# A graph network kernel: the second attention pass with the bias in the products, sigmoid from PSUM, an early running sum and three filler products a round

## The chip, the cores and the metric

The kernel runs on one core of one Trainium2 chip. The time is the device time of one execution in microseconds (us). It is given as the median of several runs.

The core has five engines with queues of their own: TensorE (PE; its weight loads are PEld), VectorE (DVE), ScalarE (ACT), GpSimd (POOL) and SyncE (SP). They wait for each other through semaphores. SP issues nearly all plain DMAs; POOL issues the indirect ones (rows by index).

## The reference

100,000 nodes with 128 channels, 50,000 edges sorted by destination, all float32. The input is normalised, goes through three layers of graph attention, is added back, normalised again, and goes through three layers of a second network (GIN). The change lies in the attention layers only:

```
h = x @ W;  s = h @ a_src;  d = h @ a_dst
e = leaky(s[src] + d[dst])                  # one score for each edge, and for each node's self loop
w = exp(e - e_max[dst]);  denom = segment_sum(w, dst)
alpha = w / (denom[dst] + 1e-16)
out = segment_sum(alpha[:, None] * h[src], dst) + bias
x = x + sigmoid(out)
```

Nodes without an incoming edge are computed in a dense pass of their own; what follows is for the nodes that have one.

## The kernel before

The work is done in stages, one behind the other. First a dense pass over all nodes computes the three attention layers as if no node had an incoming edge. Then, for each attention layer m = 0, 1, 2, two passes over the edges correct the nodes that have one: a first pass gathers the source rows by index and computes scores (only for m = 1 and 2; for m = 0 it lies beside the dense pass), a short chain on slabs of 98 x 512 makes maxima, sums and weights, and a second pass makes new node rows. The stages of the second network follow. The change touches the second pass. It is run three times and is called pass 0, pass 1 and pass 2 below.

A pass has R = 49 rounds. A round has U = 8 columns of 128 edges. `p2_round(i, ...)` is written once for each engine; in turn i an engine works on several rounds at once, as the names say: `inside(i - 1)` guards the part of the turn that is for round i-1. The order of the work is the order in which these parts are written: nothing is scheduled. `p_rounds` writes out the first three and the last turns and loops over four turns at a time between them. A round goes like this:

- DVE `early_fields` copies keys and weights of a round. PE `keys_along` (L1297) turns the keys along the free axis, eight transposes; DVE `masks` (L1792) compares them, which gives a 0/1 matrix with weights (tile pA, whose buffers are bNE and aH). ACT `diagonals` (L1047) makes eight diagonal matrices (bSW).
- PE sums the edges of a node within a column: L1311 (source rows bXs times mask) and L1312 (own rows pXd times diagonal), 8 each, into PSUM banks 2 and 3. ACT copies them to pAT (L1064).
- A node whose edges spill over a column's end needs the sum so far. DVE keeps it as a running sum pC, one scan over the last columns (L1823, L1626), round after round. PE multiplies it with W (L1305), ACT copies the 8 rows to pCW (L1053).
- One turn later PE makes the output: L1321 (pAT times W) and L1323 (an indicator matrix, tile pIN in the buffer aO, which has 1 where an edge of column u takes the carried sum u, times pCW), 8 each, into banks 4 and 5.
- DVE L1830 multiplies with 1/denom (pFL) and adds the bias (GB), eight instructions; ACT L1070 takes the sigmoid, two instructions of 512; DVE L1846 adds the old rows; POOL L864 scatters the rows by index.
- In passes 0 and 1 DVE also makes the scores of the next layer from these rows a turn later (L1808, L1810, sixteen reductions, then the copy L1814). In pass 2 DVE, POOL and ACT make the next normalisation instead (L1851 to L1863, L873 to L877, L1059).

A float32 product is run on PE as two matmuls, each with a weight load of its own, and a transpose as one. SP loads rows, indicators and stores results, each turn.

Of the kernel before, what the change touches and what calls it, by code (L numbers as in the profile page):

```python
# [22 lines left out]
P = 128  # L23
# [21 lines left out]
def gnn_program(nc, x, src, dst, attr, Ws, a_src, a_dst, gat_b, enc_w0, enc_b0, w1_0, b1_0, g_0, be_0, rm_0,  # L45
# [38 lines left out]
    ind_d = dram("ind_d", (R, U, U * P))  # L84
    gat_src = [x, x1_d, x2_d]
# [3 lines left out]
    with ExitStack() as ctx:  # L89
# [152 lines left out]
        def pair_ends(p):  # L242
# [57 lines left out]
        l_xr = sems("l_xr", 2)  # L300
        l_st = sems("l_st", 2)
        (p_fe, p_fl, p_kt, p_A, p_dg, p_ag, p_ev, p_c, p_cw, p_ce, p_rw, p_z, p_sg, p_o, p_oi, p_dt, p_dc,
         p_y, p_bs, p_bs2, p_mv, p_ve, p_rs, p_nr, p_nn) = [sem(n) for n in [
             "p_fe", "p_fl", "p_kt", "p_A", "p_dg", "p_ag", "p_ev", "p_c", "p_cw", "p_ce", "p_rw", "p_z", "p_sg", "p_o",
# [108 lines left out]
        def _(sp):  # L413
# [112 lines left out]
            for m in range(M):  # L526
# [19 lines left out]
                def p2_round(i, rr, h, m=m):  # L546
# [8 lines left out]
                    if inside(i):  # L555
                        if past(i - 2):
# [422 lines left out]
        def _(act):  # L979
# [58 lines left out]
            for m in range(M):  # L1038
# [10 lines left out]
                def p2_round(i, rr, h, m=m):  # L1049
# [90 lines left out]
        def _(pe):  # L1140
# [107 lines left out]
            for m in range(M):  # L1248
# [52 lines left out]
                def p2_round(i, rr, h, m=m):  # L1301
# [13 lines left out]
                    if inside(i - 1):  # L1315
                        pe.wait_ge(p_ce, r)
                        pe.wait_ge(l_ix[1 - s], 16 * (m * RS[1 - s] + h + (rr % 2 - 1) // 2 + 1))
                        if past(i - 2):
                            pe.wait_ge(p_z, 2 * (r - 1))
# [13 lines left out]
                keys_along(1, 1)  # L1333
                p_rounds(pe, p2_round)
# [86 lines left out]
        def _(v):  # L1421
# [239 lines left out]
            for m in range(M):  # L1661
# [133 lines left out]
                def p2_round(i, rr, h, m=m, next_s=next_s, next_d=next_d):  # L1795
# [5 lines left out]
                    if inside(i + 1):  # L1801
                        masks(i + 1, 1 - s)
                    if inside(i - 2) and m < M - 1:
# [11 lines left out]
                    if inside(i):  # L1815
                        if past(i - 2):
                            v.wait_ge(p_z, 2 * (r - 1))
# [232 lines left out]
```

## Time and profile before

| | us |
|---|---|
| median of 3 runs | 12,837.08 (12,827.12 to 12,846.73) |
| profiled execution | 12,854.73 |
| its span | 12,853.1 |
| PE, DVE, ACT, POOL busy | 7,017.4; 5,349.2; 4,324.3; 6,444.5 |
| PE weight loads busy | 5,096.5 |

The span is the time from the first to the last instruction of the profiled execution. The page also gives busy shares in 40 slices of 321 us: pass 0 lies in slices 7 to 9, pass 1 in 11 to 14, pass 2 in 15 to 18. PE's granted clock is given as a share of 2.4 GHz: 0.50 is 1.2 GHz, 1.00 is 2.4 GHz, and a value between says that both were granted in the stretch. An idle time that ends by "issue" or "remote" is one for which the profile has no other instruction to name. Times in the rows are microseconds from the span's start.

### The profile page before, as it was taken

The numbers are of one execution on the slowest core, as the hardware profiler recorded it, in microseconds if no ns is written. First come the engines' busy times: TensorE is split into PE (matmuls) and PEld (weight loads), VectorE is DVE, ScalarE is ACT, GpSimd is POOL, SyncE is SP. The second block draws the span as 40 slices with busy tenths as digits, with TensorE's granted clock in tenths as the row PEclk, the third lists the DMA queues.
The fourth block names the chain that finished last, engine by engine and source line by source line (L and its number), as shares of the span: only waits on it lengthen the run. The fifth ranks groups of instructions, "written<-read, shape, count | busy, mean of one in ns | idle before, by whom it ended". The sixth has DMA issues, their size and how long they took to land.

```text
span 12853.1 us, 167790 instructions
## 1 busy us (share of the span) xinstructions
PE 7017.4 (55%) x35048; PEld 5096.5 (40%) x35048; DVE 5349.2 (42%) x23215; ACT 4324.3 (34%) x9423; POOL 6444.5 (50%) x5862
## 2 busy tenths in 40 slices
PE   5666666750277007732222377774336887444888
PEld 2333335640266006621111255553224555333666
DVE  5666666651366226643333344441112333111544
ACT  5666663320133005532222244441113444111444
POOL 6666663456555656665666432335663333665000
PEclk9888887875688558855555688985557898555999
DMA  4555554445443555556666665666666777444998
GB/s 154 173 176 172 172 178 121 129 133 189 159 129 127 178 182 167 169 145 157 152 153 153 172 203 202 206 202 173 153 153 190 230 233 224 69 59 87 276 274 270
DMA packets 2016182, 2199.58 MB, mean 171 GB/s; under 512 B 235717, under 2 KB 1404889, under 8 KB 2009712
## 3 DMA queue, kind: packets, MB, share of 16 engines
q1 hardware_dynamic: 1698698, 1822.96, 43.4%
q0 software_dynamic: 308896, 372.55, 14.7%
q10 hardware_dynamic: 8390, 2.21, 0.1%
q14 instruction: 169, 1.38, 0.0%
q8 instruction: 29, 0.48, 0.0%
HBM read 1093.42 MB, written 1119.97 MB: 172 GB/s over the span
## 4 chain that ended last, share of the span: by engine, by line
DMA 18%; issue 11%; PE 10%; DVE 6%; another core or an unknown queue 5%; SPq 3%; POOL 2%; ACT 1%; POOLq 0%; DVEq 0%; ACTq 0%
DMA agg_d<-dO,fOI 11%; PE ps L1407 5%; DMA bXd<-agg_d 4%; PE ps L1394 2%; PE ps L1384 2%; DMA agg_d<-dO,dOI 2%; DMA aX<-y_d 2%; POOL bO L902 1%; SPq L653 1%; DVE aO L2004 1%; DVE uBS L1895 1%; DVE bXd L1977 1%; POOL agg_d L893 1%; PE ps L1382 1%
## 5 line engine op out<-in xcount | busy, mean ns | idle before, releaser
L954 POOL DMA_INDIRECT bXs<-x_d,fGI x784 | 794.7, 1014 | 1546.4 <-DMA x_d<-aH 1334.4
L893 POOL DMA_INDIRECT agg_d<-dO,fOI x784 | 1211.0, 1545 | 648.2 <-ACT dO L1082 417.7
L1082 ACT COPY dO<-ps 128x128 f32<-128x128 f32 (+1 forms) x1176 | 318.2, 271 | 2942.3 <-DMA agg_d<-dO,fOI 1644.7
L1394 PE MATMUL ps<-aS,W1X 128*128 128x512 f32 x2352 | 1206.4, 594 | 0.7 <-DMA eET<-eaT_d 0.7
L1407 PE MATMUL ps<-W,aT 128*128 128x128 f32 x9408 | 1190.3, 288 | 23.2 <-ACT aS L1116 15.9
L2012 DVE TENSOR_TENSOR aH<-ps,B 128x512 f32<-128x512 f32 x588 | 406.4, 692 | 1894.4 <-PE ps L1407 1163.4
L1363 PE MATMUL ps<-bO,bNE 128*128 128x128 f32 x1568 | 577.4, 476 | 1129.5 <-ACT dO L1082 1114.9
L1407 PEld LDWEIGHTS ps<-W,aT 128*128 128x128 f32 x9408 | 1165.6, 205 | 40.1 <-ACT aS L1116 26.3
L1122 ACT ACTIVATE aT<-ps,BNT,BNS 128x512 f32<-128x512 f32 x1176 | 881.3, 774 | 587.7 <-PE ps L1395 556.9
L1181 PE MATMUL ps<-aT,W 128*128 128x512 f32 x1176 | 776.1, 763 | 480.0 <-DVE aT L1570 382.4
L847 POOL DMA_INDIRECT bXs<-x_d,bGI x784 | 785.2, 1001 | 365.7 <-issue 248.2
L1363 PEld LDWEIGHTS ps<-bO,bNE 128*128 128x128 f32 x1568 | 385.0, 307 | 1312.6 <-issue 896.7
L893 POOL DMA_INDIRECT agg_d<-dO,dOI x392 | 616.0, 1571 | 289.2 <-ACT dO L1082 160.6
L1928 DVE TENSOR_SCALAR bNE<-ps,dK 128x128 f32<-128x128 f32 x1176 | 317.6, 343 | 1014.4 <-PE ps L1341 1012.7
L1341 PE MATMUL ps<-ident,dK 128*128 128x128 f32 x1176 | 282.4, 421 | 750.7 <-DVE dK L1923 735.5
L864 POOL DMA_INDIRECT x_d<-bO,bOI x400 | 391.3, 978 | 523.9 <-DVE bO L1846 403.7
L1384 PE MATMUL ps<-ident,aO 128*128 128x128 f32 x2352 | 430.0, 323 | 400.5 <-DVE aO L2004 390.2
L1129 ACT ACTIVATE aH<-aH 128x512 f32<-128x512 f32 x392 | 246.8, 630 | 1141.9 <-DVE aH L2012 815.4
L1212 PE MATMUL ps<-ident,SC 128*98 128x128 f32 x12 | 3.3, 430 | 1132.1 <-DVEq L1725 1132.1
L1353 PE MATMUL ps<-bO,bNE 128*128 128x145 f32 x784 | 322.2, 515 | 540.6 <-DMA bO<-gc_d,dGI 507.3
L902 POOL DMA_INDIRECT bO<-gc_d,dGI x392 | 406.4, 1037 | 396.0 <-DVE dGI L1950 284.6
L1312 PE MATMUL ps<-bSW,bXd 128*128 128x128 f32 x2352 | 583.1, 339 | 12.7 <-issue 12.5
(283 smaller groups left out, 17685.3 us busy)
## 6 DMA issues: line engine op xcount, KB each, us to landing
agg_d<-zeros SPq DMA_DIRECT2D x788, 256.0 KB
bXd<-agg_d SPq DMA_DIRECT2D x784, 256.0 KB
agg_d<-zeros SPq DMA_DIRECT2D x394, 290.0 KB
bXd<-agg_d SPq DMA_DIRECT2D x392, 290.0 KB
x_d<-aO SPq DMA_DIRECT2D x392, 256.0 KB
aX<-y_d SPq DMA_DIRECT2D x392, 256.0 KB, 4.0
x_d<-aH SPq DMA_DIRECT2D x392, 256.0 KB
aX<-x_d SPq DMA_DIRECT2D x392, 256.0 KB
```

The source lines that it names most:

```text
L847: pool.indirect_dma_start(bXs[:, s, u, :], None, gat_src[m], bass.IndirectOffsetOnAxis(ap=bGI[:, s, 0, u:u + 1], axis=0), bounds_check=n_l ...
L893: pool.indirect_dma_start(agg_d[m][u % 2], bass.IndirectOffsetOnAxis(ap=index, axis=0), dO[:, u, 0:AW[m]], None, bounds_check=agg_last, oo ...
L902: pool.indirect_dma_start(dG[:, u, 0:C], None, gin_in[0], bass.IndirectOffsetOnAxis(ap=dGI[:, u:u + 1], axis=0), bounds_check=edge_last, o ...
L954: pool.indirect_dma_start(fX[:, s, u, 0:C], None, gin_in[m], bass.IndirectOffsetOnAxis(ap=fGI[:, s, u:u + 1], axis=0), bounds_check=n_last ...
L1122: act.activation(eZ[:, k, h, :], ps[2 + 2 * k + h][:, :], ACT.Relu, bias=BNT[:, m, h:h + 1], scale=BNS[:, m, h:h + 1]).then_inc(e_zr, 1)
L1181: pe.matmul(ps[2 + k][:, :], W[:, m, :], aT[:, k, m, :], start=True, stop=True).then_inc(a_mm, 1)
L1312: mm = pe.matmul(cols(2 + u // 4, u % 4), pXd[:, rr, u, :], bSW[:, u, :], start=False, stop=True)
L1363: pe.matmul(ps[2 + u % 4][:, 0:C], dS[:, u, :], message_slot(s)[:, u, :], start=True, stop=True).then_inc(d_acc, 1)
L1384: mm = pe.transpose(ps[k][:, j * P:(j + 1) * P], eS[:, k, j, :], ident[:, :])
L1394: pe.matmul(z, W1X[:, m, h * P:(h + 1) * P], eHT[:, k, :], start=True, stop=False)
L1407: mm = pe.matmul(ps[6 + k][:, j * P:(j + 1) * P], eZ[:, k, h, j * P:(j + 1) * P], W2[:, m, h, :], start=(h == 0), stop=(h == 1))
L2012: v.tensor_tensor(eO[:, k, :, :], ps[6 + k][:, :].rearrange("p (j c) -> p j c", j=J), bias, ALU.add).then_inc(e_v, 1)
```

## The change

1. The bias goes into PSUM by the second product. The denominators are written to HBM as `den_d` at each pass start and loaded as row 32 of the indicator tile each turn; row 32 of pCW holds the bias of the layer. So L1323's product gives (indicator x carried sum) + denom x bias, with no instruction more, and 1/denom times the whole is what L1830 made.
2. The sigmoid reads PSUM with 1/denom as its scale operand: eight ACT instructions of 128x128 in place of eight on DVE and two of 128x512 on ACT. They stand ahead of `diagonals` in ACT's turn, where the two stood behind it. The semaphore p_z falls away, p_sg takes its place.
3. DVE's running sum (L1818 to L1626) stands ahead of the sixteen reductions for the next layer, where it stood behind them.
4. PE runs three products of 128x512 into the unused PSUM bank 7 behind `keys_along` in each turn. Nothing reads them.

```diff
@@ SP @@
+                        sp.dma_start(pIN[32:33, s, :], den_d[bass.ds(i, 1), :]).then_inc(l_ix[s], 16)
...
+                sp.wait_ge(z_v, ZV * (m + 1))
+                sp.dma_start(den_d.rearrange("r (h n) -> (r h) n", h=2), slU).then_inc(s_den, 16)
                 load_rows_of(0, 0)
+                sp.wait_ge(s_den, 16 * (m + 1))
                 p_rounds(sp, p2_round)
@@ ACT @@
+                    if inside(i - 1):
+                        act.wait_ge(p_fl, r)
+                        if past(i - 2):
+                            act.wait_ge(p_o, 2 * (r - 1))
+                        for u in range(U):
+                            if u % 4 == 0:
+                                act.wait_ge(p_rw, 2 * (r - 1) + u // 4 + 1)
+                            ins = act.activation(bTH[:, u, :], ps[4 + u // 4][:, (u % 4) * P:(u % 4 + 1) * P], ACT.Sigmoid,
+                                                 scale=pFL[:, 1 - s, 1, u:u + 1])
+                            if u % 4 == 3:
+                                ins.then_inc(p_sg, 1)
                     if inside(i + 1):
                         diagonals(i + 1, 1 - s)
-                    if inside(i - 1):
-                        for g in range(2):
-                            act.wait_ge(p_z, 2 * (r - 1) + g + 1)
-                            act.activation(bTH[:, 4 * g:4 * g + 4, :], bTH[:, 4 * g:4 * g + 4, :], ACT.Sigmoid).then_inc(p_sg, 1)
-
+
+                if m:
+                    act.wait_ge(p_rw, 2 * m * R)
+                act.copy(pCW[32:33, :], GB[32:33, m, :]).then_inc(p_cb, 1)
@@ PE @@
-                            pe.wait_ge(p_z, 2 * (r - 1))
+                            pe.wait_ge(p_sg, 2 * (r - 1))
...
+                    if inside(i):
+                        for k in range(3):
+                            pe.matmul(ps[7][:, :], ident[:, :], W1X[:, :, :].rearrange("p m h -> p (m h)")[:, 0:TN],
+                                      start=True, stop=True)
@@ DVE: the block of the running sum moves ahead of the reductions; L1830 goes @@
+                    if inside(i):
+                        if past(i - 2):
+                            v.wait_ge(p_sg, 2 * (r - 1))
+                        v.tensor_copy(pFL[:, s, :, :], keys[:, 4:6, bass.ds(i * U, U)]).then_inc(p_fl, 1)
...
                     if inside(i - 2) and m < M - 1:
...
-                    if inside(i - 1):
-                        for u in range(U):
-                            if u % 4 == 0:
-                                v.wait_ge(p_rw, 2 * (r - 1) + u // 4 + 1)
-                            ins = v.scalar_tensor_tensor(out=bTH[:, u, :], in0=ps[4 + u // 4][:, (u % 4) * P:(u % 4 + 1) * P],
-                                                         scalar=pFL[:, 1 - s, 1, u:u + 1], in1=GB[:, m, :], op0=ALU.mult,
-                                                         op1=ALU.add)
-                            if u % 4 == 3:
-                                ins.then_inc(p_z, 1)
```

PE at the end of a turn of pass 0, before, from the last second product to the next turn:

```order
795 L1323 MATMUL ps<-pCW,aO 128x128
796 L1297 MATMUL ps<-ident,pFE 128x128 [waits p_fe,p_A]
797 L1297 MATMUL ps<-ident,pFE 128x128 x7
798 L387 UNCONDITIONAL_BRANCH
799 L387 ISA
800 L1305 MATMUL ps<-W,pC 8x128 [waits p_c]
```

The same place of the changed kernel, where lines are numbered 16 higher:

```order
804 L1339 MATMUL ps<-pCW,aO 128x128
805 L1313 MATMUL ps<-ident,pFE 128x128 [waits p_fe,p_A]
806 L1313 MATMUL ps<-ident,pFE 128x128 x7
807 L1348 MATMUL ps<-W1X,ident 128x512 x3
808 L389 UNCONDITIONAL_BRANCH
809 L389 ISA
810 L1321 MATMUL ps<-W,pC 8x128 [waits p_c]
```

The three fillers stand between the key transposes and the product of the running sum.

DVE at the end of a turn of pass 0, before (the sixteen reductions stand ahead of the first row):

```order
637 L1814 COPY SC<-bDT 128x2x8 [waits p_dt]
638 L1818 COPY pFL<-keys 128x16 [waits p_z]
639 L1823 COPY pC<-pC 128x1 [waits p_c,p_fl,p_ev]
640 L1626 SCALAR_TENSOR_TENSOR pC<-pFL,pC,bA 128x8
641 L1830 SCALAR_TENSOR_TENSOR bTH<-ps,pFL,GB 128x128 [waits p_rw]
642 L1830 SCALAR_TENSOR_TENSOR bTH<-ps,pFL,GB 128x128 x3
643 L1830 SCALAR_TENSOR_TENSOR bTH<-ps,pFL,GB 128x128 [waits p_rw]
644 L1830 SCALAR_TENSOR_TENSOR bTH<-ps,pFL,GB 128x128 x3
645 L1843 COPY bOI<-IDX 128x8
646 L1846 TENSOR_TENSOR aT<-bTH,bXd 128x4x128 [waits p_sg] x2
```

The same turn of the changed kernel; the sixteen reductions are L1840 and L1842, rows 604 to 635:

```order
601 L1827 COPY pFL<-keys 128x16 [waits p_sg]
602 L1832 COPY pC<-pC 128x1 [waits p_c,p_fl,p_ev]
603 L1647 SCALAR_TENSOR_TENSOR pC<-pFL,pC,bA 128x8
...
636 L1846 COPY SC<-bDT 128x2x8 [waits p_dt]
637 L1855 COPY bOI<-IDX 128x8
638 L1858 TENSOR_TENSOR aT<-bTH,bXd 128x4x128 [waits p_sg] x2
```

The running sum (pC) has moved in front of the reductions, and L1830 is gone: the sums wait for p_sg only.

ACT in a turn of the loop of pass 0, before:

```order
303 L1064 COPY bA<-ps 128x512 [waits p_ag]
304 L1063 REGISTER_ALU
305 L1064 COPY bA<-ps 128x512 [waits p_ag]
306 L1045 REGISTER_ALU
307 L1047 ACTIVATE bSW<-ident,pFE 128x128 [waits p_fe]
308 L1047 ACTIVATE bSW<-ident,pFE 128x128 x7
309 L1070 ACTIVATE bTH<-bTH 128x512 [waits p_z] x2
```

The same turn of the changed kernel:

```order
297 L1070 COPY bA<-ps 128x512 [waits p_ag]
298 L1078 ACTIVATE bTH<-ps,pFL 128x128 [waits p_rw,p_o,p_fl]
299 L1078 ACTIVATE bTH<-ps,pFL 128x128 x3
300 L1078 ACTIVATE bTH<-ps,pFL 128x128 [waits p_rw]
301 L1078 ACTIVATE bTH<-ps,pFL 128x128 x3
302 L1051 REGISTER_ALU
303 L1053 ACTIVATE bSW<-ident,pFE 128x128 [waits p_fe]
304 L1053 ACTIVATE bSW<-ident,pFE 128x128 x7
```

The sigmoids have moved from behind the diagonals to ahead of them, and wait for PE's second products (p_rw).

## Rows read from the trace of the kernel before

**Rows 1.** Table by stretch: us, engines' busy time (xinstructions), clock, DMA share, GB/s.

```profile
2035.00:2810.00 775.00, 558.55 (x3626) 491.49 (x3626) 509.61 (x2745) 241.78 (x639) 382.69 (x392) 0.83 0.42 125
4802.00:5564.00 762.00, 536.25 (x3626) 495.24 (x3626) 511.40 (x2008) 377.30 (x1030) 495.62 (x539) 0.83 0.51 160
3500.00:4150.00 650.00, 472.70 (x3096) 418.53 (x3096) 436.12 (x2346) 203.88 (x540) 327.06 (x335) 0.83 0.41 129
4850.00:5500.00 650.00, 471.23 (x3182) 434.66 (x3182) 448.92 (x1761) 328.18 (x901) 431.85 (x473) 0.84 0.53 168
```

**Rows 2.** Timeline of PE, one round of pass 1: start, us, what, [idle before <-releaser].

```profile
3611.13 0.60 PE L1305 MATMUL ps<-W,pC 128*8 128x128 f32 x2
...
3617.24 0.39 PE L1321 MATMUL ps<-W,bA 128*128 128x128 f32 x2
...
3621.66 0.38 PE L1297 MATMUL ps<-ident,pFE 128*128 128x128 f32 x2 [0.68 <-issue]
...
3626.77 0.60 PE L1305 MATMUL ps<-W,pC 128*8 128x128 f32 x2
```

**Rows 3.** Table by stretch, blocks of 32 matmuls in pass 1 and pass 2.

```profile
3611.66:3617.24 5.58, 5.58 (x33) 5.58 (x33) 5.56 (x21) 1.99 (x4) 2.19 (x3) 0.64 0.24 71
3617.24:3620.98 3.74, 3.74 (x34) 3.58 (x33) 3.14 (x30) 1.43 (x5) 2.83 (x4) 1.00 0.93 285
4814.02:4817.70 3.68, 3.68 (x34) 3.68 (x33) 2.00 (x7) 2.37 (x8) 0.00 (x0) 1.00 0.89 316
```

**Rows 4.** Timeline of DVE, the same round of pass 1.

```profile
3623.23 0.17 DVE L1814 COPY SC<-bDT 128x16 f32 x1 [2.85 <-issue]
...
3626.10 2.16 DVE L1830 SCALAR_TENSOR_TENSOR bTH<-ps,pFL,GB 128x128 f32<-128x128 f32 x8 [1.21 <-remote]
```

**Rows 5.** Waits of 3437 to 4173 in pass 1: total us, times, longest.

```profile
DVE SC L1814 <- remote: 121.6, 41, 4.1
...
PE ps L1305 <- DVE pC L1626: 47.2, 19, 8.3
```

**Rows 6.** Table by stretch: starts of passes 0 and 1, two neighbouring rounds.

```profile
2035.00:2064.00 29.00, 26.13 (x204) 24.64 (x204) 19.04 (x88) 15.60 (x43) 4.72 (x5) 0.88 0.33 99
3423.00:3451.30 28.30, 25.94 (x200) 24.70 (x201) 18.43 (x83) 15.70 (x43) 4.60 (x5) 0.85 0.28 86
3657.80:3668.00 10.20, 9.65 (x76) 8.98 (x76) 9.93 (x56) 4.92 (x13) 3.88 (x4) 0.89 0.52 169
3668.00:3692.80 24.80, 13.19 (x74) 11.74 (x74) 12.48 (x63) 5.55 (x14) 11.77 (x12) 0.72 0.29 94
```

**Rows 7.** Timeline of PE in the dense pass: a product of 128x512.

```profile
1017.75 1.02 PE L1181 MATMUL ps<-aT,W 128*128 128x512 f32 x2
1018.61 0.60 PE L1189 MATMUL ps<-ident,aT 128*128 128x128 f32 x4
```

**Rows 8.** Timelines of ACT, DVE and PE, one round of pass 2.

```profile
5314.87 3.18 ACT L1059 ACTIVATE bO<-bO,bNR,bRS 128x128 f32<-128x128 f32 x8 [7.45 <-POOL bNR L877]
5317.96 1.04 ACT L1064 COPY bA<-ps 128x512 f32<-128x512 f32 x2
5318.90 2.45 ACT L1047 ACTIVATE bSW<-ident,pFE 128x128 f32<-128x128 f32 x8
...
5319.25 2.15 DVE L1830 SCALAR_TENSOR_TENSOR bTH<-ps,pFL,GB 128x128 f32<-128x128 f32 x8
...
5321.90 1.33 DVE L1846 TENSOR_TENSOR aT<-bTH,bXd 128x512 f32<-128x512 f32 x2 [0.30 <-issue]
...
5319.39 0.60 PE L1305 MATMUL ps<-W,pC 128*8 128x128 f32 x2 [2.88 <-DVE pC L1626]
```

**Rows 9.** Timelines of DVE and PE at the start of pass 2.

```profile
4795.80 3.35 DVE L1775 RECIPROCAL aYG<-aYG 98x512 f32<-98x512 f32 x1
...
4807.69 0.64 PE L1311 MATMUL ps<-bNE,bXs 128*128 128x128 f32 x2
```

More of the change, by code:

```diff
@@ L84, in gnn_program @@
     ind_d = dram("ind_d", (R, U, U * P))
+    den_d = dram("den_d", (R, U * P))
     gat_src = [x, x1_d, x2_d]
@@ L300, in gnn_program @@
         l_xr = sems("l_xr", 2)
+        s_den, p_cb = sem("s_den"), sem("p_cb")
         l_st = sems("l_st", 2)
-        (p_fe, p_fl, p_kt, p_A, p_dg, p_ag, p_ev, p_c, p_cw, p_ce, p_rw, p_z, p_sg, p_o, p_oi, p_dt, p_dc,
+        (p_fe, p_fl, p_kt, p_A, p_dg, p_ag, p_ev, p_c, p_cw, p_ce, p_rw, p_sg, p_o, p_oi, p_dt, p_dc,
          p_y, p_bs, p_bs2, p_mv, p_ve, p_rs, p_nr, p_nn) = [sem(n) for n in [
-             "p_fe", "p_fl", "p_kt", "p_A", "p_dg", "p_ag", "p_ev", "p_c", "p_cw", "p_ce", "p_rw", "p_z", "p_sg", "p_o",
+             "p_fe", "p_fl", "p_kt", "p_A", "p_dg", "p_ag", "p_ev", "p_c", "p_cw", "p_ce", "p_rw", "p_sg", "p_o",
              "p_oi", "p_dt", "p_dc", "p_y", "p_bs", "p_bs2", "p_mv", "p_ve", "p_rs", "p_nr", "p_nn"]]
@@ L1316, in p2_round @@
                         pe.wait_ge(p_ce, r)
[L1317 removed]
+                        pe.wait_ge(l_ix[1 - s], 32 * (m * RS[1 - s] + h + (rr % 2 - 1) // 2 + 1))
                         if past(i - 2):
[L1319 removed]
+                            pe.wait_ge(p_sg, 2 * (r - 1))
                         for u in range(U):
@@ L1333, in _ @@
                 keys_along(1, 1)
+                pe.wait_ge(p_cb, m + 1)
                 p_rounds(pe, p2_round)
@@ L1802, in p2_round @@
                         masks(i + 1, 1 - s)
+                    if inside(i):
+                        if past(i - 2):
+                            v.wait_ge(p_sg, 2 * (r - 1))
+                        v.tensor_copy(pFL[:, s, :, :], keys[:, 4:6, bass.ds(i * U, U)]).then_inc(p_fl, 1)
+                        v.wait_ge(p_ev, 2 * (r + 1))
+                        v.wait_ge(p_fl, r + 1)
+                        if m or past(i - 1):
+                            v.wait_ge(p_c, r)
+                        v.tensor_copy(pC[:, s, 0:1], pC[:, 1 - s, U:U + 1])
+                        scan(pC[:, s, 1:U + 1], pFL[:, s, 0, :], pAT[s][:, P - 1:U * P:P], pC[:, 1 - s, U:U + 1], ALU.mult,
+                             ALU.add).then_inc(p_c, 1)
                     if inside(i - 2) and m < M - 1:
@@ L1814, in p2_round @@
                         v.tensor_copy(SC[:, 1:3, bass.ds((i - 2) * U, U)], bDT[:, 0:2, :]).then_inc(p_dc, 1)
-                    if inside(i):
-                        if past(i - 2):
-                            v.wait_ge(p_z, 2 * (r - 1))
-                        v.tensor_copy(pFL[:, s, :, :], keys[:, 4:6, bass.ds(i * U, U)]).then_inc(p_fl, 1)
-                        v.wait_ge(p_ev, 2 * (r + 1))
-                        v.wait_ge(p_fl, r + 1)
-                        if m or past(i - 1):
-                            v.wait_ge(p_c, r)
-                        v.tensor_copy(pC[:, s, 0:1], pC[:, 1 - s, U:U + 1])
-                        scan(pC[:, s, 1:U + 1], pFL[:, s, 0, :], pAT[s][:, P - 1:U * P:P], pC[:, 1 - s, U:U + 1], ALU.mult,
-                             ALU.add).then_inc(p_c, 1)
-                    if inside(i - 1):
-                        for u in range(U):
-                            if u % 4 == 0:
-                                v.wait_ge(p_rw, 2 * (r - 1) + u // 4 + 1)
-                            ins = v.scalar_tensor_tensor(out=bTH[:, u, :], in0=ps[4 + u // 4][:, (u % 4) * P:(u % 4 + 1) * P],
-                                                         scalar=pFL[:, 1 - s, 1, u:u + 1], in1=GB[:, m, :], op0=ALU.mult,
-                                                         op1=ALU.add)
-                            if u % 4 == 3:
-                                ins.then_inc(p_z, 1)
                     if inside(i - 1):
@@ L1868, in _ @@
                 p_rounds(v, p2_round)
+                v.wait_ge(s_den, 16 * (m + 1))
                 if m < M - 1:
```

## The prediction

> **What bounds the kernel now.** The page's table of busy shares names no bound: no engine is above 55%, and POOL's half is spread over all stages. So the first view is the table by stretch for the three edge passes, which are all that the change touches: pass 0 has 775 us, pass 2 has 762 and pass 1 lies between, some 2,300 us of the span of 12,853 [rows 1]. Everything outside them is charged at zero, except the pass starts, below. Each pass is 49 rounds, so a round lasts 15 to 16 us.
>
> The second view is the timeline of one round of the middle pass. PE starts a round at 3611.13 and the next at 3626.77, 15.6 us. Its two blocks of products run without a gap, 5.6 us (granted clock 0.64 of 2.4 GHz) and 3.7 us (1.00) [rows 3]. Then come eight key transposes; what they wait for was done long ago, yet there are gaps of some 0.7 us between them, and the block lasts until 3626.8 [rows 2]. VectorE stalls at the same time: its small copy L1814 stands 2.85 us with nothing late, the first L1830 another 1.21 us [rows 4]. Two engines with separate queues are held together, and the third view, the waits, says that this is the rule: L1814 waits in 41 of 47 rounds, and only part of PE's wait (47.2 us in 19 rounds) goes to the running sum [rows 5].
>
> The fourth view tells what kind of hold it is. I count instructions, as the table by stretch gives them (matmuls, weight loads, VectorE, ScalarE, GpSimd). In the first 29.0 us of pass 0 there are 544, in the first 28.3 us of pass 1 there are 532; that is 19 a microsecond, and only then do the pauses begin. One round at 3657.8 passes without a pause: 225 instructions in 10.2 us; the next takes 24.8 us for 237. Together they come to 35.0 us, two ordinary rounds and 4 us [rows 6]. What is gained in one round is paid back in the next. In the steady stretches of pass 1 and pass 2, very different in their work, the rates are 9,414/650 = 14.5 and 9,499/650 = 14.6 instructions a microsecond [rows 1]. I read this as a cap of about 14.5 instructions a microsecond over all engines, behind a store that lets bursts through. It is a reading, not a fact: that the two rates agree could be chance, for pass 2 also has a chain of its own length (below).
>
> **The change part by part.** Own time: the profiled execution has 12,854.7 us, 1.6 outside its span and 17.6 above the median of 12,837.1. I work out a difference and add it to the median.
>
> *Instructions.* A float32 product is run as two matmuls with a weight load each, a transpose as one of each. Per round before: PE 148 (3,626 of each kind in 49 rounds), VectorE 56, ScalarE 13, GpSimd 8 = 225; pass 2: 148+41+21+11 = 221 [rows 1]. Three fillers: +6 matmuls, +6 loads = +12. Eight L1830 off VectorE: −8. Two sigmoids of 512 become eight of 128: +6. Net +10. At 14.5 a microsecond that is 0.69 us a round; a pass has some 46 rounds behind its first burst, so 3 × 46 × 0.69 = +95 us.
>
> *Fillers.* One 128x512 float32 product takes PE 0.86 us at the full clock (from 1017.75 to the next instruction at 1018.61) [rows 7], and about twice that at 1.2 GHz; three are 2.6 to 5.2 us a round. They stand behind the key transposes and ahead of the running-sum product. In pass 2 PE waits 2.88 us there for the running sum [rows 8], so they fit. In passes 0 and 1 they lie where PE is being held anyway. Under the cap they run inside the hold and cost their 12 instructions; without that cover they cost up to 5.2 us.
> The first products of a round take 5.58 us at a granted clock of 0.64 (part at 1.2, part at 2.4 GHz, behind a stretch in which PE had gaps), and 3.68 at 1.00 [rows 3]. The Trainium skill, TensorE: Matmul & The Clock Gate, section "What's actually happening", says that the lower clock is the resting state and activity lifts it. By that rule fillers would save up to 1.9 us a round of PE time and spend 2.6, a net loss of 0.7 us even if PE were the bound; under the cap neither counts.
>
> *Sigmoid from PSUM.* It takes L1830 (2.15 us a round) and its hand-over to ScalarE away. A sigmoid of 128x128 from PSUM is not in the trace; the nearest rows are eight L1047 in 2.45 us (one scale operand, 0.31 each) and eight L1059 in 3.18 us (scale and bias operand, 0.40 each) [rows 8]. So eight sigmoids cost 2.4 to 3.2 us; I take 2.8. In passes 0 and 1 ScalarE is busy for 242 of 775 us [rows 1], which hides it. In pass 2 it is on the chain: rstd on GpSimd, eight L1059 (5314.87 to 5318.05), two L1064 (to 5319.0), then before: scan and L1830 (5319.25 to 5321.40), first L1846 at 5321.90, 2.9 us behind the copies, both sums done by 5323.23. After: four sigmoids (1.4 us), four more while the first sum runs, second sum from 2.8+0.2 to 3.7 us behind the copies, against 4.2 before [rows 8]. The chain of pass 2 shortens by 0.5 us (bounds: 0.1 and 0.9, by 3.2 and 2.4). I charge nothing for it, since under the cap that round has to be 0.69 us longer; without the cap it is 49 × 0.5 = −25 us (−5 to −44).
>
> *Diagonals behind the sigmoids.* Eight L1047 now wait for the second products. First diagonal is ready some 2.5 us behind the last second product; PE meanwhile has transposes (1.0), fillers (2.6) and the running-sum product (0.4). Hidden by 1.5 us; if the fillers were gone it would cost up to 1.1.
>
> *Early running sum.* The scan stands ahead of sixteen reductions, so PE's 47 us of waits in pass 1 (a microsecond a round) and as much in pass 0 can go: bounds 0 and −98 us. Under the cap it turns into hold; I take 0.
>
> *Bias row.* No instruction more in the products; one 4 KB DMA a round on SP, whose data is used a round later: 0. At each pass start SP now waits for the denominators before it loads rows. Their reciprocal ends at 4799.15, the first products begin at 4807.69 [rows 9]: 8.5 us for a write and two loads. I take +1 us a pass, bounds 0 and 5.
>
> Sum: 95 + 3 − 0 = +98, rounded +100: **12,940 us**.
>
> **The rivals.**
> *Faster: the hold is a matter of time, not of count.* The pauses come behind the sixteen reductions and in a busy stretch of DMA. If they stay 5 us a round whatever is issued, the waits for the sum and L1830 come off: about 1 us in each of 98 rounds [rows 5] and 0.5 in 49, −98 − 25 = −120: 12,715. For it: pauses sit at the same place of every round. Against it: the pair of 10.2 and 24.8 us; and PE has to find room for 2.6 us of fillers. If the pauses vanished altogether, 98 rounds would fall from 15.6 to about 11.3 (PE: 0.4+3.7+3.6+1.0+2.6), −420: 12,420.
> The Trainium skill, NOTIFIC — the notification-queue block, section "Constraints, capacities, measured rates", says that recording an instruction costs its engine nothing; no row here tells what is behind the hold. By it a count of recorded instructions would be no reason for a limit, and the faster rival would stand.
> *Slower by more: fillers are serial on PE.* If the hold falls on the transposes first and the fillers run after it, a round of passes 0 and 1 is 0.5+3.7 to 5.6+3.7+5.8+2.6 = 16.3 to 18.2, say +1.7 × 98 = +165 and pass 2 +33: 13,035.
> *No change:* if VectorE's instructions weigh more in the cap than PE's, −8 outweighs much of +12: within 26 us. Passes 0/1 with 56 on VectorE are held harder than pass 2 with 41, which speaks for some of this.
>
> **How the numbers follow.** Cap 0.50 (12,940; its own range 12,890 to 12,990), serial fillers 0.13, faster with pauses 0.22, pauses gone 0.05, no change 0.10. Faster or slower means by over 0.2%, about what a measurement of this kernel can tell: faster 0.27, same 0.12 (with a share of the cap case), slower 0.61. Range 12,715 to 13,050: it leaves out the vanished pauses, a part of the faster case and a thin end above.
>
> **What would show it.** Right: PE 3,920 matmuls a pass, 233 to 235 instructions a round, a steady rate still at 14.3 to 14.7, rounds of 16.2 us in passes 0 and 1 and 15.7 in pass 2; PE's idle time at the running-sum product gone but transposes or fillers with gaps that nothing explains. Wrong: a rate above 15 in a steady stretch (no cap, faster), or rounds over 16.8 with fillers unbroken behind paused transposes (serial). In pass 2, L1059 to L1846 should show eight sigmoids of 0.30 to 0.40 us.

## The result, and the profile after

The changed kernel takes 12,949.1 us (median of 4, 12,935.2 to 12,992.6) against 12,839.9 for the kernel before, measured beside it: a ratio of 1.0092 (95% interval 1.0066 to 1.0118). It is slower by 109 us; 12,940 was forecast. The profiled execution is the longest of the four, 43 us above the median, with a span of 12,990.8 us. Of its engines PE is busy for 7,321.4 us (7,017.4 before), VectorE for 5,030.6 (5,349.2), ScalarE for 4,466.0 (4,324.3) and GpSimd for 6,476.8 (6,444.5).

The first look is at the same kind of stretches as in [rows 1]. Table by stretch of the changed kernel: the three passes whole, then a steady part of pass 1 and of pass 2:

```profile
2036.00:2890.00 854.00, 686.86 (x3932) 536.56 (x3932) 402.01 (x2359) 290.92 (x933) 386.67 (x396) 0.86 0.39 116
3494.00:4360.00 866.00, 689.36 (x3938) 545.25 (x3938) 403.32 (x2363) 291.63 (x933) 388.52 (x398) 0.85 0.36 115
4960.00:5680.00 720.00, 576.28 (x3920) 470.49 (x3920) 413.95 (x1618) 424.56 (x1324) 513.48 (x535) 0.96 0.55 173
3560.00:4210.00 650.00, 528.05 (x2992) 415.22 (x2990) 305.41 (x1814) 223.00 (x720) 291.55 (x300) 0.86 0.37 116
5000.00:5600.00 600.00, 492.20 (x3369) 401.34 (x3368) 357.33 (x1403) 362.13 (x1134) 442.64 (x464) 0.98 0.57 180
```

From their first round to their last, passes 0 and 1 are longer by 73 and 83 us, and pass 2 is shorter by 41 (table of the experiments, below). The instructions a microsecond, the same 14.5 and 14.6 in both passes before, are now 8,816/650 = 13.6 in pass 1 and 9,738/600 = 16.2 in pass 2. Fewer instructions a microsecond where the kernel got slower and more where it got faster is not one cap for both. So the forecast was right in its total and wrong in its mechanism.

One number of the profile carries the rest of this text. GpSimd issues eight scatters a round (DMAs that write rows to HBM by index), 0.97 us each and 0.30 apart; then it waits for VectorE's next sums. A chain below is one round's eight scatters, and the hold is the time in which the other engines all but stand with nothing late. The waits of GpSimd in pass 1, of the kernel before (3423 to 4185) and of the changed kernel (3494 to 4360): total us, times, longest.

```profile
POOL x_d L864 <- DVE bO L1846: 190.2, 24, 56.2
POOL x_d L864 <- DVE aT L1846: 119.7, 24, 5.5
```

```profile
POOL x_d L870 <- DVE bO L1858: 225.1, 24, 58.1
POOL x_d L870 <- DVE aT L1858: 169.8, 25, 8.5
ACT aYG L1070 <- remote: 166.9, 31, 8.4
DVE pC L1832 <- ACT bA L1070: 165.4, 20, 9.8
ACT bA L1070 <- remote: 157.2, 29, 8.8
```

Without the longest, which is the one ahead of the pass's first scatter, GpSimd waits 253.7 us before and 336.8 after: 83.1 us more. Pass 1 grew by 83.0 (table below). What is left of a pass, 478 us, is the same in both: 48 chains of eight scatters, 9.96 us each. A round of passes 0 and 1 is a chain of scatters plus the time from its end to the next sums, 5.3 us before and 7.0 after (253.7 and 336.8 over 48). Why little of the next round gets done beside the chain is seen in one round. Timeline of GpSimd in the round of [rows 2 and 4], before:

```profile
3614.44 0.97 POOL L864 DMA_INDIRECT x_d<-aT,bOI  x1 [5.38 <-DVE aT L1846]
...
3622.16 0.97 POOL L864 DMA_INDIRECT x_d<-aT,bOI  x1 [0.30 <-issue]
3623.43 0.97 POOL L864 DMA_INDIRECT x_d<-aT,bOI  x1 [0.30 <-issue]
```

Beside [rows 2 and 4]: the chain starts at 3614.4, PE's gaps begin at 3621 and end at about 3626, 1.5 to 2 us behind the end of the chain. PE had started its round at 3611.13, 3.3 us ahead of the chain, and all 32 products were through before the hold. Now a round of the changed kernel, all engines:

```profile
4052.90 0.97 POOL L870 DMA_INDIRECT x_d<-aT,bOI  x1 [6.70 <-DVE aT L1858]
4054.11 0.39 PE L1321 MATMUL ps<-W,pC 128*8 128x128 f32 x2
...
4059.67 0.74 PE L1339 MATMUL ps<-pCW,aO 128*128 128x128 f32 x2
4060.05 0.59 ACT L1070 COPY aYG<-ps 128x512 f32<-128x512 f32 x1 [5.26 <-remote]
...
4061.85 0.97 POOL L870 DMA_INDIRECT x_d<-aT,bOI  x1 [0.30 <-issue]
4062.89 0.27 PE L1337 MATMUL ps<-W,bA 128*128 128x128 f32 x1 [0.92 <-issue]
...
4064.39 0.59 ACT L1070 COPY aYG<-ps 128x512 f32<-128x512 f32 x1 [3.75 <-remote]
4064.87 2.29 ACT L1078 ACTIVATE bTH<-ps,pFL 128x128 f32<-128x128 f32 x8
4065.00 0.15 DVE L1832 COPY pC<-pC 128x1 f32<-128x1 f32 x1 [9.35 <-ACT aYG L1070]
4065.22 0.28 DVE L1840 CUSTOM_DVE_ANT_0 bTL<-aT,VR 128x128 f32<-128x128 f32 x1
...
4067.45 2.74 PE L1348 MATMUL ps<-W1X,ident 128*128 128x512 f32 x6
...
4069.36 1.29 DVE L1858 TENSOR_TENSOR bO<-bTH,bXd 128x512 f32<-128x512 f32 x2
4070.11 0.39 PE L1321 MATMUL ps<-W,pC 128*8 128x128 f32 x2
...
4070.86 0.97 POOL L870 DMA_INDIRECT x_d<-bO,bOI  x1 [8.03 <-DVE bO L1858]
```

PE starts 1.2 us behind the chain's start instead of 3.3 ahead. Over pass 1, PE starts a round 0.1 us ahead of the chain in the median, against 3.5 before (starts of L1321 or L1305 against the first scatter of each chain). The fillers have eaten the head start: without them it is 3.9 (e1). So here its second products (from 4058.1) run into the hold, and ACT's copy of first products that PE's records show as done at 4058.3 comes at 4064.39. On VectorE the running sum waits 9.35 us for that copy, and the sixteen reductions, now queued behind it, run from 4065.2 to 4068.7, behind the hold; in the round of the kernel before, above, they were over at 3620.4, when the hold began. Only then come the sums and the next chain.

The lost head start is not the price by itself. In e4 (below) PE starts 3.2 us behind the chain in the median, and pass 1 takes 741 us; there the reductions stand ahead of the instruction that waits for the late copy.

### The profile page after: what moved, and what is told of

Its sections match the earlier page's. It is cut to its first block, busy times and chain, and to the rows that moved or that the text cites. A ratio compares the mean times of both kernels' runs of the same rounds, so it can differ in the third digit from the quotient of the medians.

```text
span 12990.8 us, 169822 instructions
## 1 busy us (share of the span) xinstructions
PE 7321.4 (56%) x35930; PEld 5173.9 (40%) x35930; DVE 5030.6 (39%) x22039; ACT 4466.0 (34%) x10308; POOL 6476.8 (50%) x5862
## 3 DMA queue, kind: packets, MB, share of 16 engines
q0 software_dynamic: 308896, 372.55, 14.5%
## 4 chain that ended last, share of the span: by engine, by line
DMA 18%; PE 10%; issue 10%; DVE 6%; another core or an unknown queue 6%; SPq 3%; POOL 2%; ACT 1%; DVEq 0%; POOLq 0%; ACTq 0%
DMA agg_d<-dO,fOI 11%; PE ps L1428 5%; DMA bXd<-agg_d 3%; PE ps L1415 2%; PE ps L1405 2%; DMA aX<-y_d 2%; DMA agg_d<-dO,dOI 2%; POOL bO L908 1%; DVE bXd L1990 1%; SPq L659 1%; DVE aO L2017 1%; DVE uBS L1908 1%; POOL agg_d L899 1%; PE ps L1403 1%
## 5 line engine op out<-in xcount | busy, mean ns | idle before, releaser
L1428 PE MATMUL ps<-W,aT 128*128 128x128 f32 x9408 | 1201.1, 290 | 24.9 <-ACT aS L1132 13.4
L1020 ACT ACTIVATE aS<-ps,GBC 128x512 f32<-128x512 f32 x588 | 403.6, 686 | 555.3 <-PE ps L1197 474.1
```

What stands on the lines that cost most here:

```text
L1020: act.activation(aS[:, k, :], ps[2 + k][:, :], ACT.Sigmoid, bias=GBC[:, m:m + 1]).then_inc(a_sg, 1)
L1428: mm = pe.matmul(ps[6 + k][:, j * P:(j + 1) * P], eZ[:, k, h, j * P:(j + 1) * P], W2[:, m, h, :], start=(h == 0), stop=(h == 1))
```

## The experiments

Of each kernel the table gives the ratio to the kernel before (95% interval), and the us between the first and the last product of the running sum (L1321, L1305 before) in each pass: 48 rounds. The passes are those of the profiled execution, which for the changed kernel and for e7 lies 43 and 35 us above the median. The kernel before measured 12,829 to 12,847 us beside most of them, but 12,765 beside e9, e10 and e11, which shared another chip; compare those by ratio. e5, e8, e11 and e12 leave a part of the result out, which their expectations name.

| | ratio | pass 0 | pass 1 | pass 2 |
|---|---|---|---|---|
| before | 1 | 735 | 732 | 717 |
| changed kernel | 1.0092 | 808 | 815 | 676 |
| e1 no fillers | 1.0013 (1.0003 to 1.0023) | 758 | 759 | 672 |
| e2 fillers alone | 1.0129 (1.0112 to 1.0146) | 813 | 814 | 718 |
| e3 six small fillers | 1.0120 (1.0103 to 1.0137) | 777 | 790 | 762 |
| e4 late sum | 0.9984 (0.9974 to 0.9993) | 748 | 741 | 673 |
| e5 no reductions | 0.9963 (0.9949 to 0.9977) | 745 | 725 | 676 |
| e6 late sum, no fillers | 0.9940 (0.9923 to 0.9956) | 723 | 724 | 673 |
| e7 e6 + 24 SP increments | 0.9940 (0.9923 to 0.9956) | 731 | 728 | 678 |
| e8 half loads | 1.0083 (1.0066 to 1.0100) | 800 | 815 | 671 |
| e9 e6 + 12 GpSimd copies | 0.9949 (0.9932 to 0.9966) | 716 | 711 | 663 |
| e10 e6, grouped reductions | 0.9861 (0.9840 to 0.9882) | 658 | 639 | 662 |
| e11 e6, wide products | 0.9933 (0.9914 to 0.9953) | 707 | 703 | 660 |
| e12 half the scatters | 0.9642 (0.9626 to 0.9658) | 543 | 547 | 642 |

**e1, the changed kernel without fillers.**

```diff
-                        for k in range(3):
-                            pe.matmul(ps[7][:, :], ident[:, :], W1X[...][:, 0:TN], start=True, stop=True)
```

> The changed kernel without its three filler products. Serial fillers (in passes 0 and 1 PE is held first and runs the fillers, 2.7 us a round, afterwards): rounds of passes 0 and 1 fall from 17.3 to about 14.6 us, 98 x 2.7 = 265 us, to about 12,690; pass 2 stays at 14.1 us a round. Count (a round pays for its instructions, 12 fewer at the 13.6 a microsecond that passes 0 and 1 now show): 98 x 0.9 = 88 us, to about 12,860. Hold of fixed length that covers the fillers: no change, 12,950.

12,847.3 us: by the ratios 0.79% or 101 us less than the changed kernel, all of it in passes 0 and 1 (−1.1 us a round); pass 2 hardly moves. By the number that is the count theory's 12,860; e3 tells them apart.

**e2, the kernel before with the fillers alone.** The same four lines added to it.

> The kernel before with the three filler products alone. Serial fillers: passes 0 and 1 gain 1.7 to 2.7 us a round, 98 rounds, +165 to +265, so 13,005 to 13,105; pass 2 hides them in PE's wait of 2.9 us for the running sum. Count: 12 more in all 147 rounds at 14.5 a microsecond, +0.83 us each, +122, 12,960, a third of it in pass 2. Covered by the hold: 12,840.

12,990.6 us, +162, all of it in passes 0 and 1 (+78 and +82): just under the low end of serial fillers (+165), and nothing in pass 2. In its timeline of a round of pass 1 the next round starts behind the chain, as above:

```profile
3687.98 0.97 POOL L864 DMA_INDIRECT x_d<-bO,bOI  x1 [8.15 <-DVE bO L1850]
...
3689.67 0.39 PE L1305 MATMUL ps<-W,pC 128*8 128x128 f32 x2
...
3699.73 0.58 ACT L1064 COPY bA<-ps 128x512 f32<-128x512 f32 x1 [3.90 <-remote]
```

**e3, the changed kernel with six fillers of 128x32.**

```diff
-                        for k in range(3):
-                            pe.matmul(ps[7][:, :], ident[:, :], ...[:, 0:TN], start=True, stop=True)
+                        for k in range(6):
+                            pe.matmul(ps[7][:, 0:32], ident[:, :], ...[:, 0:32], start=True, stop=True)
```

> The changed kernel with six fillers of 128x32 in place of three of 128x512: twice the instructions (24 against 12 a round), a fraction of PE's time (12 matmuls of some 0.07 us against 6 of 0.45). If time on PE is what is paid for: close to the run without fillers, 12,700 to 12,750. If instructions are paid for: above the changed kernel by 12 / 13.6 = 0.9 us in 98 rounds, 13,035.

12,980.8 us, between the two in passes 0 and 1, and a surprise in pass 2, which becomes 86 us longer than with the large fillers. Steady part of pass 2, table by stretch:

```profile
4940.00:5640.00 700.00, 522.03 (x3716) 497.77 (x3715) 363.98 (x1424) 381.67 (x1173) 449.55 (x477) 0.84 0.50 157
```

Neither theory has this: by time they cost nothing, by count (15.0 instructions a microsecond here, 16.2 above) the large ones should already be over the limit. PE's granted clock is lower here (0.84 against 0.98), but that isn't the price: without fillers pass 2 takes 672 us at 0.87 (e1). The number of instructions seems to weigh something, but there is no one rate.

**e4, the changed kernel with the running sum back behind the reductions**, and **e6, the same without fillers.**

```diff
-                    if inside(i):        # pFL, pC, scan: ahead of the reductions
+                    if inside(i):        # the same block, behind them
```

> The changed kernel with the running sum back behind the sixteen reductions. If the early sum has taken PE's waits for it away (47 us a pass before) and nothing took their place: +94 us, about 13,040, all of it in passes 0 and 1. If the wait was only turned into hold or lies beside the fillers: 12,950, no change. Pass 2 has no reductions and stays as it is by either.

12,807.3 us: not slower but, by the ratios, 1.08% or 139 us faster than the changed kernel. The early sum costs; of the two expectations one had +94 and the other no change.

> The late-sum kernel without the fillers: 223 instructions a round in passes 0 and 1. Limit on events at 15.2 a microsecond: 14.7 us a round against 15.5, 98 x 0.8 = -78, 12,730; pass 2 stays at 14.0. If PE's time counts and fillers lie in PE's wait for the late sum: no change, 12,807. If the fillers' activity is what holds the clock up (granted 0.92 in the late-sum kernel) and that is worth more than their events: a round gets longer, up to 15.8 as in the kernel without fillers, +30, 12,835.

12,767.2 us, 0.6% below the kernel before, near the mean of the first two expectations (12,730 and 12,807). GpSimd's waits in pass 1, of e4 (3433 to 4210) and of e6 (3410 to 4170):

```profile
POOL x_d L870 <- DVE bO L1858: 180.7, 24, 58.4
POOL x_d L870 <- DVE aT L1858: 128.2, 24, 6.8
```

```profile
POOL x_d L870 <- DVE bO L1854: 175.9, 25, 56.9
POOL x_d L870 <- DVE aT L1854: 119.4, 24, 5.6
```

Without the longest that is 250.5 and 238.4 us, against 336.8: the pass is again the chains (486 to 491 us) plus this wait. The three fillers, 162 us alone (e2) and 101 beside the early sum (e1), cost 0.44% or 57 us beside the late one (e4 against e6). Why they are so much cheaper there no run separates.

**e5, the changed kernel without the reductions.**

```diff
-                        for u in range(U):
-                            v.tensor_tensor_reduce(bTL[:, u, :], ...)
-                            ins = v.tensor_tensor_reduce(dO[:, u, 0:C], ...)
+                        ins = v.tensor_copy(bDT[:, 0:2, :], bOs[s][:, 0:2, 0:U])
```

> The changed kernel without the sixteen reductions of passes 0 and 1 (one small copy stands for them; the next layer's scores are left out). All theories see VectorE's load fall. Limit on events over all engines: 15 fewer of 235 instructions; at 15.2 a microsecond (the rate at which the small-filler and late-sum kernels run in all their passes) a round is 220 / 15.2 = 14.5 us against 16.9, so 98 x 2.4 = 235 us less, 12,715. Hold caused by the reductions themselves: passes 0 and 1 run unheld, 11.2 us a round (PE's work with fillers), -560, 12,390. Hold caused by data traffic: the holds stay, 15 instructions on an engine that is not the bound give nothing, 12,930 to 12,950.

12,798.2 us, 1.29% or 166 us below the changed kernel, between all of them. The expectation miscounts: each reduction is two instructions in the trace, so 31 go and the limit would give 204/15.2 = 13.4 us a round; the round is 15.3, at 13.3 instructions a microsecond, with holds in nearly all. Neither a fixed rate nor the reductions make the hold. What it gains is near what e4 gains, 139, which fits the reading above: in both, no reductions stand between the late copy and the sums.

**e7, e6 with 24 semaphore increments a round on SP**, and **e9, e6 with 12 copies on GpSimd.**

```diff
+                        for k in range(24):
+                            sp.sem_inc(s_gate, 1)
```

> The late-sum kernel without fillers, with 24 semaphore increments a round on SyncE, which is idle most of the round; nobody waits for them, and they cost no other engine an instruction. Limit on events over all engines: 24 more events a round; if one of them weighs as much as an instruction, +1.6 us in passes 0 and 1 (+155), and pass 2 is pushed over the limit too, from 14.0 to about 15.5 (+70): +225 over the kernel without them. If it weighs half, +80 to +100. Holds that come from PE, VectorE, the data traffic or each engine's own queue: no change.

```diff
+                            for u in range(12):
+                                ins = pool.tensor_copy(bJK[:, u:u + 1], mhalf[:, 0:1])
```

> The late-sum kernel without fillers (12,767), with 12 copies of 128x1 a round on GpSimd behind the scatter of passes 0 and 1, where it is idle for 4.5 to 5 us; nobody waits for them. If instructions of every compute engine draw on one store, +12 cost what 12 fillers' instructions cost between the pairs measured so far, 0.4 to 1.0 us a round: 12,807 to 12,867. If only the instructions of PE, VectorE and ScalarE are held and count (GpSimd's scatters keep their step of 1.27 us through every hold): 12,767, no change.

0.9940 and 0.9949 against 0.9940: no cost that can be told. Of e9, table by stretch, GpSimd with 801 instructions where e6 has about 325:

```profile
3450.00:4050.00 600.00, 457.90 (x2981) 411.94 (x2980) 349.85 (x1930) 231.56 (x761) 383.64 (x801) 0.84 0.42 135
```

That is 15.8 instructions a microsecond. If there is a store, the instructions of GpSimd and SP do not draw on it.

**e8, the changed kernel with half the row loads.**

```diff
-                    sp.dma_start(bXs[:, s, :, :], by_round(xs_d, i)).then_inc(l_in[s], 16)
+                    sp.dma_start(bXs[:, s, 0:4, :], by_round(xs_d, i)[:, 0:4, :]).then_inc(l_in[s], 16)
```

> The changed kernel with only columns 0 to 3 of the two row loads of each round (the other four keep old data): 512 KB less of some 2 MB a round, same instructions. Hold caused by data traffic: passes 0 and 1 lose a good part of their hold of some 5 us, 17 to 14 us a round or below, -290 or more, 12,650 or below. Limit on events: nothing changes but for the fewer DMA packets, 12,900 to 12,950. Hold by the reductions: 12,950.

12,944.6 us; the interval includes the changed kernel's ratio. GB/s fell from 116 and 115 to 87 in passes 0 and 1 and the holds stayed. The row loads aren't the cause.

**e10, e6 with grouped reductions.**

```diff
+                        for t, (prod, vec) in enumerate([(bTL[:, :, :], next_d), (dO[:, :, 0:C], next_s)]):
+                            v.tensor_tensor(prod, bOs[s][:, :, 0:C], vec.unsqueeze(1).to_broadcast([P, U, C]), ALU.mult
+                                            ).then_inc(p_pr, 1)
+                        for t, prod in enumerate([bTL[:, :, :], dO[:, :, 0:C]]):
+                            v.wait_ge(p_pr, 2 * (r - 2) + t + 1)
+                            ins = v.tensor_reduce(bDT[:, t, :], prod, axis=mybir.AxisListType.X, op=ALU.add)
```

> The late-sum kernel without fillers, with the sixteen reductions (32 instructions, a reduction and a read of its sum each, 3.4 us of VectorE) replaced by two products of 128x1024 and two sums over them: 4 instructions, and by the width about 4.6 us of VectorE. Instruction count: 28 fewer a round, at 0.034 to 0.09 us each 1.0 to 2.5 us a round in passes 0 and 1, 12,530 to 12,670. Time on VectorE: 1.2 us more a round, 12,767 where its slack hides it, up to 12,885 where not. Pass 2 has no reductions and stays at 14.0 us a round.

Ratio 0.9861, 0.8% below e6 or 101 us, with more time on VectorE (402.0 us in 580 against 356.3 in 620 for e6): the low end of the count theory. It computes the whole reference, and is the fastest kernel here that does. About half of its rounds in passes 0 and 1 take 11.4 us or less and are hardly held; some are long. In 62 of these passes' 96 rounds the next chain follows within 0.5 us, so a chain beside the work does not hold it every time. Rows of PE, GpSimd, VectorE and ScalarE from one of 28.3 us:

```profile
3764.74 0.38 PE L1321 MATMUL ps<-W,pC 128*8 128x128 f32 x2
...
3775.93 0.97 POOL L870 DMA_INDIRECT x_d<-aT,bOI  x1 [0.30 <-issue]
...
3777.68 0.27 PE L1328 MATMUL ps<-bSW,bXd 128*128 128x128 f32 x1 [1.13 <-issue]
...
3782.32 0.97 POOL L870 DMA_INDIRECT x_d<-aT,bOI  x1 [0.30 <-issue]
3782.58 0.37 PE L1327 MATMUL ps<-aH,bXs 128*128 128x128 f32 x1 [1.74 <-issue]
3783.98 1.37 DVE L1809 TENSOR_SCALAR bNE<-ps,pFE 128x128 f32<-128x128 f32 x4 [8.43 <-issue]
...
3786.12 0.26 ACT L1059 COPY pCW<-ps 8x128 f32<-8x128 f32 x1 [13.57 <-remote]
```

GpSimd runs from one round's chain into the next without a break, and PE, VectorE and ScalarE all but stand; VectorE goes on 0.7 us behind its last scatter, PE and ScalarE 2 to 3 us behind. PE's single matmuls start 2.8, 2.1, 2.8 and 0.7 us apart. The long round of [rows 6] is the same case: GpSimd has 12 instructions in it, and 4 in the short one. A second effect shows: 85 single scatters take 1.5 to 3.2 us in place of 0.97, where they meet VectorE's products of 128x1024. From another stretch:

```profile
2125.14 3.13 POOL L870 DMA_INDIRECT x_d<-aT,bOI  x1 [0.30 <-issue]
...
2125.08 1.22 DVE L1825 TENSOR_TENSOR bTL<-aT,VR 128x1024 f32<-128x1024 f32 x1
2126.22 1.22 DVE L1825 TENSOR_TENSOR dO<-aT,VR 128x1024 f32<-128x1024 f32 x1
2127.35 1.21 DVE L1829 TENSOR_REDUCE bDT<-bTL 128x8 f32<-128x1024 f32 x1
```

The scatter ends at 2128.27, 0.83 us behind the second product and in the middle of a sum; 82 of the 85 end 0.84 us behind a product, while the scatters that start within a sum keep 0.97. The Trainium skill, Advanced Engine Details and Errata, section "Mode Summary", notes that VectorE's second SBUF port is shared with GpSimd, and that GpSimd's instructions and VectorE's two-port ones block each other. The trace agrees as far as the scatters wait out a product that reads two SBUF tensors (bTL and dO from aT and VR) and not a sum that reads one; whether that product is one of the two-port instructions no run shows. Nothing of the kind is seen for the hold of PE.

**e11, e6 with wide second products.**

```diff
-                            mm = pe.matmul(cols(4 + u // 4, u % 4), pIN[...], pCW[:, :], start=False, stop=True)
                             if u % 4 == 3:
+                                mm = pe.matmul(ps[4 + u // 4][:, :], pIN[...], W1X[...][:, 0:TN], start=True, stop=True)
```

> The late-sum kernel without fillers, with the eight second products of 128x128 (32 PE instructions, 3.5 us of matmul at the full clock beside the weight loads) replaced by two of 128x512 into the same banks (8 instructions, about 1.8 us by the filler's 2.7 us for three). The carried sums are left out of the result. Instruction count on PE: 24 fewer, at 0.034 to 0.09 us each 0.8 to 2.1 us a round in passes 0 and 1, 12,560 to 12,690; pass 2 unchanged. A hold of fixed length a round, or one that comes from elsewhere than PE: no change but for what PE's shorter block lets start earlier, 12,720 to 12,770.

Ratio 0.9933 against 0.9940, which can't be told apart, for 24 PE instructions fewer a round. PE also starts 2.2 us ahead of the chain in the median, against 0.9 us behind in e6, and gains nothing by it. PE's part of the count theory falls.

**e12, the changed kernel with every second scatter left out.**

```diff
                     for u in range(U):
+                        if u % 2 == 1:
+                            continue
```

The waits for the scatters' landing are halved to match.

> The changed kernel with only the even columns scattered, four scatters a round of 128 rows in place of eight, in all three passes (the odd columns' rows are left out). Before this run the holds were seen to begin some 5 us into a chain of scatters and to end within 2 to 3 us of its end, and to last some 9 us where two rounds' scatters ran without a break. Hold tied to the chain of scatters (10.2 us of a round): with 5.1 us of them the rounds of passes 0 and 1 fall from 16.9 us to between 11.1 (what unheld rounds of this kernel take) and 12.5, that is 98 x 4.4 to 5.8 = 430 to 570 us less than the changed kernel, 3.3 to 4.4% below it; its ratio to the kernel before falls from 1.009 to between 0.965 and 0.976. Limit on instructions of all engines: four fewer, -0.3 us a round, ratio 1.007. Hold by PE, VectorE or the row loads: no change, 1.009. Pass 2, which is not held: 14.1 us a round, or a little less where GpSimd comes earlier to the normalisation.

12,372.5 us, ratio 0.9642, 4.5% below the changed kernel with the same instructions otherwise. Rounds of 11.3 and 11.4 us, as expected for a hold tied to the scatters; the ratio is a little beyond because pass 2 is 35 us shorter too. Table by stretch, passes 0 and 1:

```profile
2080.00:2560.00 480.00, 475.20 (x3383) 389.74 (x3382) 339.86 (x2025) 242.90 (x804) 164.53 (x168) 1.00 0.54 159
3250.00:3750.00 500.00, 491.76 (x3486) 402.06 (x3486) 352.89 (x2103) 253.10 (x835) 167.43 (x172) 1.00 0.50 157
```

PE is busy for 99% of the first stretch at the full clock, and 9,762 instructions in 480 us are 20.3 a microsecond. With four scatters a round there is no hold in passes 0 and 1: PE's waits with no named cause are below 1 us in every round. So the hold needs the eight scatters.

## Why the prediction was right in its number and wrong in its reasons

- *The cap of 14.5 instructions a microsecond* was the step that failed. Rates of 15.8 (e9), 16.2 and 20.3 (e12) lie above it, and passes at 13.3 (e5) and 13.6 are held though they lie below; 14.5 and 14.6 before were the chance that the text named. (The sum 9,414 is 9,413, which changes nothing.) Its term of +95 has no counterpart. In its place: a round of passes 0 and 1 is a chain of scatters of 10 us, during whose later part PE, VectorE and ScalarE are held until about 2 us behind it, plus what is left of the path to the next sums (5.3 us before, 7.0 after). Two of the signs that the text named for a wrong forecast came: a rate above 15 (16.2 in pass 2), and rounds over 16.8 (16.8 and 17.0), but the paused instructions are PE's second products and not the transposes. The clue stood in [rows 6], in the column of GpSimd, which was counted and not read.
- *Fillers.* "In passes 0 and 1 they lie where PE is being held anyway" was wrong. They run behind the hold, so they delay the next round's products against the chain. Taken alone they cost 162 us (e2), out of the changed kernel 101 (e1), and beside the late sum 57 (e4 against e6). What they give back came as counted: the first products of a round, 5.58 us at a granted clock of 0.64, take 3.67 us at 1.00 behind the fillers (4054.43 to 4058.10). The fillers themselves take 2.7 us from 4067.45 in the round shown, and 5.0 us from 4049.16 just ahead of it, at a granted clock of 0.54, most of it at the lower level of 1.2 GHz. The rival with serial fillers had +165 in passes 0 and 1, which is what the fillers alone cost (+78 and +82, e2). The changed kernel's passes 0 and 1 grew by 73 + 83 = 156, but with the early sum's price and the other parts' gain in it. That rival's rounds of 16.3 to 18.2 us are what was measured (16.9), its +33 in pass 2 is not.
- *Early running sum.* Taken at 0 between 0 and −98; it costs 139 us with fillers (e4) and 94 without (e1 against e6, 0.73%). PE's waits for the sum did go, as forecast. But the reductions now queue behind an instruction that waits up to 10 us for a held copy. The text named what waits for the sum, and not what is queued behind its wait. Fillers and early sum together cost 1.52% or 195 us (after against e6), about half or more of it the sum's, whichever of the two is taken out first.
- *Pass 2* was forecast at +0.69 us a round under the cap or −0.5 without; it was −41/48 = −0.85. The chain, taken with bounds 0.1 and 0.9, now reads, in the timeline of a round (to be held against [rows 8]):

```profile
5302.76 3.18 ACT L1065 ACTIVATE bO<-bO,bNR,bRS 128x128 f32<-128x128 f32 x8 [6.19 <-POOL bNR L883]
5305.85 1.04 ACT L1070 COPY bA<-ps 128x512 f32<-128x512 f32 x2
5306.79 2.16 ACT L1078 ACTIVATE bTH<-ps,pFL 128x128 f32<-128x128 f32 x8
5307.95 0.69 DVE L1858 TENSOR_TENSOR aT<-bTH,bXd 128x512 f32<-128x512 f32 x1 [0.49 <-ACT bTH L1078]
...
5309.38 0.46 PE L1327 MATMUL ps<-aH,bXs 128*128 128x128 f32 x2 [1.72 <-ACT bSW L1053]
```

  Eight sigmoids take 2.16 us, under the lower bound of 2.4. Sums are done at 5309.67, 2.8 us behind the copies' end at 5306.89, against 4.2: this piece is shorter by 1.4 us, beyond the upper bound of 0.9. The diagonals, which were to be hidden by 1.5 us, now keep PE for 1.72; it has the time, since fillers end at 5306.5 and the round has 14.1 us.
- *Bias row and pass starts* weren't tried by themselves. All that is left without fillers and early sum (e6) is worth −0.6%, 77 us, of which pass 2 has 44. That gives the whole change: −77 for e6, +57 for the fillers, +139 for the early sum, together +119, where the ratio of the whole change gives +118.

So two errors met, and that the total came out was luck: +95 was added for a limit that isn't there, and the true costs in passes 0 and 1 (+156) less the gain in pass 2 (−41) come to nearly the same, 115 us. (These are of the two profiled executions, which differ by 138 us; the medians differ by 109.)

**What stays open.** That the hold needs the chain of scatters is shown (e12). Through what, is not, nor that the chain is enough by itself. In the hold PE and VectorE start single instructions some 0.7 us apart or a multiple of it (1.4, 2.1, 2.8) while GpSimd keeps its step of 1.28. Pass 2, with the same eight scatters in 14 us, is held far less: PE's waits with no named cause at the second products (L1337, L1339) are 34.7 us in 4960 to 5680 of the changed kernel, against 106.9 in 3494 to 4360 of pass 1. How many instructions the others issue beside the chain matters in some way: 28 fewer on VectorE free half of the rounds (e10, though there the scatters are slower too), 12 more small ones on PE bring pass 2 into the hold (e3), yet 24 fewer on PE change nothing (e11), nor do more on GpSimd (e9) and SP (e7). Whether a scatter's descriptors, its rows written to HBM or its completions count was not separated. Nor was the recording of the instructions itself: every execution here has a span and a granted clock, so each was recorded in some form, and none can show whether the hold is there without it. Fetching of code is an unlikely cause: two DMA queues carry instructions, with only 29 and 169 packets in the whole span before, 30 and 169 after.

## What to carry to other kernels

Before adding work behind a stall, find what the stall is tied to, by reading every column of the stretch: here the idle time of PE and VectorE was the shadow of a chain on a third engine, and work put behind it was not hidden. When an instruction is moved ahead in an engine's queue, price what is then queued behind its wait, in the worst round. A rate that comes out equal in two stretches is worth one run that changes it before anything is built on it; and where rows go out by index, fewer scatters may be worth more than any change to the engines that seem busy (here half of them took 4.5% off).

## What the runs showed of the hardware

- Eight scatters of 128 rows keep GpSimd for 10 us, and in the later part of such a chain PE, VectorE and ScalarE are held to single instructions some 0.7 us or a multiple of it apart, in the rounds shown until 1.5 to 3 us behind its end (VectorE once 0.7); with four scatters a round PE ran at 99% (e12). In e10 half of the rounds escape this.
- One VectorE reduction of 128x128 with a running total is two instructions, 0.28 and 0.08 us, one each 0.21 us; sixteen take 3.5 us, and four grouped instructions of 128x1024 take 4.6 (1.21 each, 1.13 apart) and still made the kernel 0.8% faster (e10).
- Eight sigmoids of 128x128 from PSUM take 2.16 to 2.3 us, 0.27 each.
- GpSimd's scatter takes up to 3.2 us in place of 0.97 beside VectorE's products of two SBUF tensors of 128x1024, and ends 0.84 us behind them; a sum over one tensor of 128x1024 does not delay it (e10).
- 24 semaphore increments a round on SP and 12 small copies on idle GpSimd cost nothing that can be measured.
